# Softmax sums of an attention kernel: inverted in a 128-row block behind three DMAs instead of in place

## The reference

```python
Q, K, V = split_heads(query @ Wq.T + bq), split_heads(key @ Wk.T + bk), split_heads(value @ Wv.T + bv)
scores = jnp.einsum('bhqd,bhkd->bhqk', Q, K) / np.sqrt(Hd)
attn = jax.nn.softmax(scores, axis=-1)
out = jnp.einsum('bhqk,bhkd->bhqd', attn, V)
out = out.transpose(0, 2, 1, 3).reshape(B, S, D)
return out @ Wo.T + bo
```

## Time and profile before

| | |
|---|---|
| median of 3 runs | 1872.41 us (1872.25 to 1873.85) |
| profiled execution, its own time | 1873.76 us |
| profiled execution, its span | 1872.0 us |
| mean granted TensorE clock | 0.957 |
| attention stage | up to about 1065 us |
| PE busy over the span | 1692.8 us (90%) |
| DVE busy over the span | 1334.0 us (71%) |

### The profile page before, as it was taken

One profiled execution on the slowest core, in us unless ns is written; L12 is line 12 of the kernel. 1 busy time (PEld: TensorE's weight loads), 2 busy tenths in 40 slices (PEclk: granted clock), 3 DMA queues, 4 the chain that ended last, 5 costly groups with the idle time before them and its releaser, 6 DMA issues. The chain is left out here.

```text
span 1872.0 us, 31059 instructions
## 1 busy us (share of the span) xinstructions
PE 1692.8 (90%) x10405; PEld 1247.7 (67%) x10405; DVE 1334.0 (71%) x2330; ACT 691.5 (37%) x1317; POOL 469.3 (25%) x643
## 2 busy tenths in 40 slices
PE   4799999999999989999998729999999999999996
PEld 4555565555555555555554218998998989889895
DVE  4577667675766676767555587788888888888864
ACT  2254353443533533434334204242434433434221
POOL 3112112121121121121210202434343334233322
PEclk8999999999999999999998859999999999999998
DMA  5333233341332333413212142354544636636322
GB/s 185 86 91 112 85 90 86 94 113 52 112 104 61 100 106 103 112 53 102 75 57 79 46 145 74 106 201 127 191 142 176 218 111 218 212 120 221 96 75 79
DMA packets 104565, 216.04 MB, mean 115 GB/s; under 512 B 26704, under 2 KB 27728, under 8 KB 104400
## 3 DMA queue, kind: packets, MB, share of 16 engines
q1 hardware_dynamic: 77488, 135.53, 22.9%
q0 software_dynamic: 26912, 78.47, 13.3%
HBM read 204.19 MB, written 37.36 MB: 129 GB/s over the span
## 5 line engine op out<-in xcount | busy, mean ns | idle before, releaser
L595 DVE TENSOR_REDUCE negmax<-max_ps 128x2 f32<-128x1024 f32 x256 | 311.6, 1217 | 150.5 <-PE max_ps L376 148.9
L480 ACT ACTIVATE pt<-work 128x512 f32<-128x512 f32 x512 | 278.0, 597 | 327.4 <-PE work L388 325.5
L1188 PE MATMUL gu_ps<-xgT_hi,wg_hi 128*128 128x256 f32 x1248 | 354.8, 284 | 0.0
L1188 PE MATMUL gu_ps<-xgT_hi,wg_lo 128*128 128x256 f32 x1248 | 351.5, 282 | 0.0
L1188 PE MATMUL gu_ps<-xgT_lo,wg_hi 128*128 128x256 f32 x1248 | 351.4, 282 | 0.0
L376 PE MATMUL max_ps<-ks,qs 96*128 96x512 f32 x512 | 190.4, 454 | 56.9 <-DVE negmax L595 39.6
L1188 PEld LDWEIGHTS gu_ps<-xgT_hi,wg_hi 128*128 128x128 f32 x1248 | 235.3, 189 | 0.0
L1188 PEld LDWEIGHTS gu_ps<-xgT_lo,wg_hi 128*128 128x128 f32 x1248 | 235.3, 189 | 0.0
L1188 PEld LDWEIGHTS gu_ps<-xgT_hi,wg_lo 128*128 128x128 f32 x1248 | 235.2, 188 | 0.0
L376 PEld LDWEIGHTS max_ps<-ks,qs 96*128 96x128 f32 x512 | 85.2, 196 | 139.6 <-issue 74.1
L1248 ACT ACTIVATE sig<-gate 128x256 f32<-128x256 f32 x156 | 65.1, 417 | 304.2 <-DVE gate L1300 302.1
(11 more groups left out here) (192 smaller groups left out, 3078.6 us busy)
## 6 DMA issues: line engine op xcount, KB each, us to landing
raw_g<-w_gate_up SPq DMA_DIRECT2D x39, 2048.0 KB
raw_d<-w_down SPq DMA_DIRECT2D x39, 1024.0 KB
ks<-k_hi SPq DMA_DIRECT2D x256, 64.0 KB, 2.1
qs<-q_hi SPq DMA_DIRECT2D x256, 64.0 KB, 2.7
bd<-b_down SPq DMA_DIRECT2D x39, 256.0 KB
x_in<-x SPq DMA_DIRECT2D x8, 1024.0 KB, 5.8
ctxT_raw<-ctx_t SPq DMA_DIRECT2D x8, 1024.0 KB, 6.5
ks<-k_lo POOLq DMA_DIRECT2D x128, 64.0 KB, 2.3
```

Of the source, the lines that this page charges most:

```text
L480: e.activation(pt[k % 2][:, h, :], in_work("exp", u, k, h)[:, :], ACT.Exp, scale=scale).then_inc(exped.sem, 1)
L595: e.tensor_reduce(negmax[:, u % 2, n:n + 2], max_ps[:, :, :], AX.X, ALU.max, negate=True).then_inc(maxed.sem, 1)
L1188: ins = e.matmul(gu_ps[n % GU_BANKS][:, part, :], wg[s][pw][:, k, cols], xgT[s][px][:, k, :], start=(k == 0 and m == 0), stop=(k == KD - 1 ...
```

## The change

For the units 0 to 30 the inversion is no longer made in place. Four keys take the place of the four `norm`:

- `gather` (r1, SyncE's queue): when the sums are copied, one row of `o_sum` a head, 512 sums, goes by DMA into the 32 rows of that head in the new block `sums_c`, 16 to a row. These are 4 DMAs of 2 KB;
- `invert` (r2): VectorE inverts the 128x16 block into `inv_c`; SyncE's queue waits for it and stores it to DRAM, 8 KB;
- `spread` (r3): SyncE's queue waits for the store's landing and reads each head's 512 inverses back over that head's 32 partitions of `o_sum`, with 4 DMAs of 64 KB;
- `divide` (r4): VectorE waits for these and makes one product of 128x512.

The last unit, 31, is normalised as before.

```diff
-                    at(2, ("norm", s - 1, 0))
-                    at(3, ("norm", s - 1, 1))
-                    at(4, ("norm", s - 1, 2), ("norm", s - 1, 3))
+                    at(1, ("gather", s - 1))
+                    at(2, ("invert", s - 1))
+                    at(3, ("spread", s - 1))
+                    at(4, ("divide", s - 1))
...
+            def invert(u):
+                e.wait_ge(sums_in.sem, sums_in[u])
+                if u:
+                    e.wait_ge(inv_stored.sem, inv_stored[u - 1])
+                e.reciprocal(inv_c[:, :], sums_c[:, :]).then_inc(inverted.sem, 1)
+
+            def divide(u):
+                b, c = divmod(u, C)
+                e.wait_ge(copied.sem, copied[u, 0])
+                if c == 0 and b:
+                    e.wait_ge(out_made.sem, out_made[b - 1, T - 1])
+                e.wait_ge(inv_in.sem, inv_in[u])
+                e.tensor_tensor(oT[:, c, :], o_sum[:, 0, :], o_sum[:, 1, :], ALU.mult).then_inc(divided.sem, 1)
...
+            def gather_sums(u):
+
+                e.wait_ge(copied.sem, copied[u, 1])
+                if u:
+                    e.wait_ge(inverted.sem, inverted[u - 1])
+                for h in range(GROUP):
+                    e.dma_start(sums_c[HD * h:HD * (h + 1), :], o_sum[HD * h:HD * h + 1, 1, :]).then_inc(sums_in.sem, 16)
+
+            def store_inverses(u):
+                e.wait_ge(inverted.sem, inverted[u])
+                if u >= 2:
+                    e.wait_ge(inv_in.sem, inv_in[u - 2])
+                e.dma_start(inv_dram[u % 2].rearrange("h (p n) -> (h p) n", p=HD), inv_c[:, :]).then_inc(inv_stored.sem, 16)
+
+            def spread_inverses(u):
+                e.wait_ge(inv_stored.sem, inv_stored[u])
+                for h in range(GROUP):
+                    e.dma_start(o_sum[HD * h:HD * (h + 1), 1, :], inv_dram[u % 2, h].partition_broadcast(HD)).then_inc(inv_in.sem, 16)
```

More of the change, by code:

```diff
@@ L47, in __init__, with attention_stage @@
             over[bank] = (mark, event)
-def attention_stage(nc, x, ctx_t, w_t, bq, bk, bv, bo, router_wt, router_b, out, xln_dram, logits, ident):
+def attention_stage(nc, x, ctx_t, w_t, bq, bk, bv, bo, router_wt, router_b, out, xln_dram, inv_dram, logits, ident):
     B, S, D = x.shape
@@ L89, in attention_stage @@
         o_sum = sb("o_sum", [P, 2, S])
+        sums_c = sb("sums_c", [P, S // HD])
+        inv_c = sb("inv_c", [P, S // HD])
         rw_cols = sb("rw_cols", [P, C, HD])
@@ L223, in attention_stage @@
         m_sent = Mark(sem("m_sent"), units, 32)
+        sums_in = Mark(sem("sums_in"), units[:-1], 16 * GROUP)
+        inv_stored = Mark(sem("inv_stored"), units[:-1], 16)
+        inv_in = Mark(sem("inv_in"), units[:-1], 16 * GROUP)
         x_turned = Mark(sem("x_turned"), TOKENS)
@@ L256, in attention_stage @@
         m_lo_made = Mark(sem("m_lo_made"), units)
-        inverted = Mark(sem("inverted"), [(u, t) for u in units for t in range(T)])
-        divided = Mark(sem("divided"), [(u, t) for u in units for t in range(T)])
+        inverted = Mark(sem("inverted"), [*units[:-1], *[(units[-1], t) for t in range(T)]])
+        divided = Mark(sem("divided"), [*[(u, T - 1) for u in units[:-1]], *[(units[-1], t) for t in range(T)]])
         x2_made = Mark(sem("x2_made"), TOKENS)
@@ L413, in project_out @@
                     if k == C - 1 or t == 0:
-                        e.wait_ge(divided.sem, divided[b * C + k, T - 1 if k < C - 1 else t])
+                        e.wait_ge(divided.sem, divided[b * C + k, t if b * C + k == units[-1] else T - 1])
                     ins = e.matmul(to[:, :], oT[:, k, t * P:(t + 1) * P], wo[:, k, :], start=(k == 0), stop=(k == C - 1))
@@ L600, in max_lo @@
                                 ALU.subtract).then_inc(m_lo_made.sem, 1)
+            def invert(u):
[10 more added lines that the diff above has]
+                e.tensor_tensor(oT[:, c, :], o_sum[:, 0, :], o_sum[:, 1, :], ALU.mult).then_inc(divided.sem, 1)
             def normalise(u, t):
-                b, c = divmod(u, C)
+                c = u % C
                 cols = slice(t * P, (t + 1) * P)
@@ L607, in normalise @@
                 e.wait_ge(copied.sem, copied[u, 0])
-                if c == 0 and b:
-                    e.wait_ge(out_made.sem, out_made[b - 1, T - 1])
                 e.wait_ge(inverted.sem, inverted[u, t])
@@ L625, in on_dve @@
                     v_out(*what)
+                elif kind == "invert":
+                    invert(*what)
+                elif kind == "divide":
+                    divide(*what)
                 elif kind == "norm":
@@ L763, in on_sp @@
                     send_max(*what)
+                elif kind == "gather":
+                    gather_sums(*what)
+                elif kind == "invert":
+                    store_inverses(*what)
+                elif kind == "spread":
+                    spread_inverses(*what)
                 elif kind == "load_x":
@@ L1488, in build @@
     xln_dram = nc.dram_tensor("xln_dram", (B, S, D + E), F32, kind="Internal").ap()
+    inv_dram = nc.dram_tensor("inv_dram", (2, GROUP, S), F32, kind="Internal").ap()
     with ExitStack() as ctx:
@@ L1508, in _ @@
                 e.wait_ge(ident_made, 2)
-        attention_stage(nc, x, ctx_t, (wq_t, wk_t, wv_t, wo_t), bq, bk, bv, bo, router_wt, router_b, out, xln_dram[:, :, 0:D], logits, ident)
+        attention_stage(nc, x, ctx_t, (wq_t, wk_t, wv_t, wo_t), bq, bk, bv, bo, router_wt, router_b, out, xln_dram[:, :, 0:D], inv_dram, logits, ident)
         F2, F = w_gate_up.shape[2], w_down.shape[1]
```

## The result

The changed kernel takes 2019.7 us (median of 4 runs, 2017.0 to 2024.5), the kernel before 1872.3 us (median of 4, 1869.9 to 1873.9): a ratio of 1.078, with a 95% interval of 1.076 to 1.081. It is slower by 147 us. The forecast was 2035 us, with a range of 1950 to 2125. Medians and ratios leave out one run of experiment 10, of 2211.8 us, in which the granted clock was 0.73 where the kernel's other runs had 0.94.

A forecast was written before the change was run, and what follows sets the result against it. TensorE was taken to set the pace, VectorE's relief being mostly slack. Late steps of 51.6 + 24.5 + 34.4 + 23.2 us and 27 for the clock, 161 us, on 1873.8 gave 2035 us, range 1950 to 2125.

The forecast's parts named there:

- The signs named in the forecast: VectorE's DMA waits some 300 us, TensorE's reduction waits over 100, r6 late in four step kinds, VectorE's busy time down 131.
- What VectorE is spared: Inversions and products of 164.9 us shrink to 34.2, a gain of 131 us for VectorE, almost all of it slack.
- Issues and landings: On SyncE's queue each DMA takes 0.62 us to issue; gather lands in 1.8 us, store 2.0, reads 2.1.
- The rule on DRAM: DRAM access of 2 us at high load would delay the eight c = 1 stores: 2051 us, not in the sum.
- c = 1: Eight steps: reads queue behind a 1 MB load, r6 5.9 us late, some returns at r0; net 4.3 us, 34.4 in all.
- c = 3: Six steps with both loads: gather lands behind them, r4 7.7 us late, r6 8.6 us late; 51.6 us in all.
- c = 0: Seven steps: gather behind the keys' DMAs, store behind the queries'; r6 3.5 us late, 24.5 us in all.
- c = 2: Eight steps: store behind the queries' DMAs, r6 2.9 us late, 23.2 us in all; the ruler takes 1.8 off each.
- TensorE's clock: Waits lower TensorE's granted clock: two more losses of 1.7 us per four steps, 27 us on top.
- The small DMAs are not held up by the loads: Rival: the chain's small DMAs land without delay from loads in c = 3 and c = 1; 2012 us, chance 0.12.
- The waits feed on each other: Rival: landings at the long end, 2.8 us, and more clock loss; 2108 us, up to 2149, chance 0.15.
- The chain is covered: Rival: transfers arrive in time and VectorE's relief counts, at most 38.2 us of TensorE's waits; some 1835 us, chance 0.04.

The follow-up runs named there:

- experiment 10: The changed kernel with its nine DMAs a unit on GpSimd's queue and the loads of ctxT_raw and of the residual moved to r4: 1965.5 us.
- Experiment 4: The changed kernel without the gather and its wait, VectorE inverting 16 columns of the sums in place; store, reads and their wait stay: 2001.5 us.
- Experiment 9: The changed kernel with the 1 MB residual load of the c = 3 steps moved from r0 to r4, behind the reads: 2008.0 us.
- experiment 11: The changed kernel, nine DMAs on GpSimd's queue, ctxT_raw and residual loads in r4, x_in load in r2, its statistics r6, normalisation r7: 1943.2 us.

## Why the prediction was right

**The cause** stood as forecast. The chain of three dependent transfers misses its place in VectorE's order, and VectorE's wait reaches TensorE through the reduction. Experiment 2 keeps the nine DMAs (the reads a quarter as large) and takes the waits away: +11 us instead of +147. Experiment 1 takes both away: -7 us. The signs named in the forecast came too: VectorE waits 309 us for DMAs (some 300 forecast), TensorE 150.5 us for the reduction (over 100).

**What VectorE is spared**: 164.9 us before; now 23.5 + 7.8 + 3.7 + 1.2 (the last two for unit 31) = 36.2, so 129 us against 131. The product of 128x512 took 756 ns, not the 686 of the nearest row; the inversion 250 against 248. That this is slack is what experiment 1 shows: of at most 38.2 us, TensorE's waits fall by 20.4 and the time by 7. The forecast allowed 1835 us for a covered chain; 1864 is what it would have been.

**Issues and landings**: the store landed in 1.6 us (2.0 forecast), the gather in 1.7 (1.8), the reads in 2.1 (2.1), these medians over all steps. The issue of the four reads took 1.72 us, 0.43 each and not 0.62, but the four pieces of the gather behind the loads 3.37 us, 0.84 each. These two errors have opposite signs.

**The rule on DRAM**, weighed in the forecast and left out of its sum: over the 31 stores of the changed kernel the landing took 1.4 to 3.1 us, with 1.6 as the median, and 3.1 was reached once, ahead of the load of the step with c = 1 shown above. Over the eight stores with c = 1 the median is 1.6 too. So the 2 us at high load (the Trainium skill, page "DMA: Bandwidth & Descriptors", section "Latency and other measured facts") are borne out at most by 1.5 us more in that one store, and the 2051 us would have been farther off than 2035. Experiment 4's 5.6 us are of another kind, a wait behind loads.

**c = 3**: 8.6 us forecast, 9.05 measured. In the step shown r4 was to be 7.7 us late and was 7.75; `sums_in` was forecast for 413.8 + 51.73 = 465.5, and came at 465.8. Over the six steps r4 was 8.5 us late. Experiment 9 confirms the term by its part: one load less ahead, 2.4 us less a step.

**c = 0**: 3.5 forecast, 3.56 measured, but by another path, and the agreement is in part luck. r4 waits as forecast (1.7 us a step, 1.8 us late). r6 then waits in none of the seven steps. The late product meets the projection out, which the forecast had dismissed with "three of its four chunks can be done before it comes": TensorE does the three and waits for the fourth, 5.1 us in five steps, and its matmuls from r4 on are slower. A step with c = 0, the projection and r6:

```profile
658.79 1.13 PE L423 MATMUL work<-wo,oT 128*128 128x512 f32 x2 [0.70 <-DVE oT L622]
659.93 0.74 PE L384 MATMUL max_ps<-ks,qs 96*128 96x512 f32 x2
```

**c = 2**: 1.1 forecast and 0.76 measured. At r6, with what returned at r0, nothing was left (-0.2 us a step); the 0.76 us arise behind it.

**c = 1 was too small by 10 us**, 6.1 forecast (of which no row gives the last 0.2) and 7.36 measured. That the loss is the second wait's alone is shown by experiment 4, where c = 1 costs 7.45 without any gather. The lateness of r6 was forecast well: 5.9 us, and 5.6 in the mean of the eight steps (6.7 in the step shown, r5 at 481.09 before and at 546.03 after, where the reads were complete at 553.7 and not at the 488.0 of the forecast, 552.9 on this clock). What the forecast lacked comes behind r6, 1.75 us a step, and is the clock. In the step shown TensorE took 7.8 us from r6 to the step's end instead of 5.2:

```profile
555.68 1.22 PE L384 MATMUL max_ps<-ks,qs 96*128 96x512 f32 x2 [6.69 <-DVE negmax L603]
...
563.50 0.28 PE L390 MATMUL work<-ident,negmax 128*16 128x128 f32 x1
```

**TensorE's clock was mis-sized, and counted in the wrong place.** "Two more such losses per four steps, 27 us" was added on top of the lateness of the steps. The loss itself is even larger, 34.4 us of longer matmuls. In the 29 steps of the table, 14 us of them fall ahead of r6 and 19 behind it, and the steps grow by 19 us behind r6. What comes behind the last wait costs in full; what comes ahead of it can shorten a wait instead. The step with c = 3 shows how: at the lower clock r4 to r5 takes 1.9 us more, while r6 cannot start before the chain is through in any case; the slow matmuls shorten the wait before r6 to 1.32 us and not the step. In c = 1 the half speed follows after the last wait. So the clock was 8 us too large in the sum; the lateness of r6, 134 us in the forecast and 125 in the traces, was 9 too large; 2 us that no term had came outside these steps. 8 + 9 - 2 is the 15 us between 2035 and the measured time. No run held the clock still, so this split is read from the traces and not tried by itself.

**Rivals.** "The small DMAs are not held up by the loads" (2012 us) lies nearer to the measured time than 2035 does, and is nevertheless refuted: DMAs of 2 KB took 6.5 us to land behind the loads. A total that fits does not decide between mechanisms; the landing of the pieces does. "The waits feed on each other" did not come: outside the loads the median landings stayed at 1.6 to 2.1 us. "The chain is covered" would have been experiment 1.

## What to carry to other kernels

An engine with slack in its sum has none at a given place of its order: before work is moved off it into a chain of transfers, work out for each step when the last transfer lands and which instruction stands behind the one that waits for it. A small DMA in series is priced by what is in flight when it is issued or is issued within a microsecond of it, loads of another queue too, and by what waits ahead of it in its own queue, and not by its median; keep it apart from loads by a wait or by one queue's order, not by a place in a list. Time at the lower clock of TensorE was added here only where no later wait swallowed it.

## What the runs showed of the hardware

**A load in flight delays small DMAs of its own queue and of the other.** 2 KB behind two 1 MB loads on the same queue: 6.5 us to land, instead of 1.7. 64 KB on GpSimd's queue, with the loads on SyncE's: 7.1 us (experiment 11), instead of the 2.5 of all its reads.

**A sum on GpSimd can stop a product on VectorE.** In the next to last step with c = 3 of the kernel before, which loads the residual alone, the residual's addition meets VectorE's third product:

```profile
917.15 4.54 POOL L671 TENSOR_TENSOR x<-x,bo_rows 128x2048 f32<-128x2048 f32 x1 [0.49 <-DMA x<-x]
917.77 4.08 DVE L611 TENSOR_TENSOR oT<-o_sum 128x128 f32<-128x128 f32 x1
```

That product takes 4.08 us where others take 0.29, and ends just after GpSimd's instruction (921.85 against 921.69). The Trainium skill, page "SBUF — State Buffer", section "Who interferes with whom", states it: a VectorE instruction with two inputs in SBUF contends with a GpSimd instruction that reads SBUF, since its second input comes through the read interface that the two share; the lock is exclusive, and the order of issue decides who blocks. The trace agrees: GpSimd had started 0.6 us earlier. In experiment 1 the one product of that step starts 0.5 us ahead of the same addition and takes its ordinary time:

```profile
906.47 0.68 DVE L619 TENSOR_TENSOR oT<-o_sum 128x512 f32<-128x512 f32 x1
```

This step is 7.0 us shorter there, the largest single gain of that run; how much of the 7.0 is the port was not tried by itself. In the last such step of experiment 1 GpSimd starts first, at 1012.2, and the same product, 1.1 us behind it, takes 4.07 us.
